# Six instead of three buffers for inverse degrees, residual rows and output rows in the pipelines after the two graph layers, with the output stores issued two steps later

## The reference, cut to what matters

```python
def _sage_layer(x, src, dst, deg_inv, Wl, bl, Wr):
    agg = segment_sum(x[src], dst) * deg_inv
    h = agg @ Wl.T + bl + x @ Wr.T
    norm = maximum(norm_of_row(h), EPS)
    return relu(h / norm)

h = _sage_layer(x, src, dst, deg_inv, Wl0, bl0, Wr0)
h = _sage_layer(h, src, dst, deg_inv, Wl1, bl1, Wr1)
out = layernorm(x + h)          # (v - mean) / sqrt(var + eps), over the 64 features
```

## Time and profile before

| what | us |
|---|---|
| median of 3 runs | 7693.83 |
| lowest and highest of them | 7691.86, 7711.77 |
| the profiled execution: its time | 7695.09 |
| the profiled execution: span from first to last instruction | 7693.3 |
| in it: edge stage of the first network and what precedes it, about | 0 to 5190 |
| node stage c, then the edge stage of layer 0, about | 5190 to 6406 |
| node stage after layer 0 | 6406 to 6492 |
| edge stage of layer 1 | 6492 to 7533 |
| node stage after layer 1, the last | 7533 to 7693.3 |

### The profile page before, as it was taken

The page is one execution under the profiler, slowest core; times in us unless marked ns, Lnnn a source line. Parts: engine busy times, 40 slices in busy tenths (PEclk is TensorE's granted clock), DMA queues, the critical chain, the costliest instruction groups (busy, mean ns, idle before and its releaser), DMA issues. The chain is left out here.

```text
span 7693.3 us, 142775 instructions
## 1 busy us (share of the span) xinstructions
PE 6764.5 (88%) x40296; PEld 5280.2 (69%) x40296; DVE 4537.4 (59%) x17372; ACT 2229.5 (29%) x4883; POOL 5906.4 (77%) x4715
## 2 busy tenths in 40 slices
PE   5998999989889998898999988987999996999993
PEld 4777877878778877787788877865555554555552
DVE  5777777777777777633333333336666664666663
ACT  2222222222222222222222222226333334333333
POOL 5888888888888888888888888864788784877873
PEclk7777777776777777766666677668999996999995
DMA  4333333333333333322222222223333334323342
GB/s 132 34 35 33 34 35 34 34 34 34 34 34 34 34 34 33 33 28 27 28 27 27 27 28 27 27 38 120 75 73 76 75 71 72 74 74 77 75 71 53
DMA packets 718022, 374.05 MB, mean 49 GB/s; under 512 B 550672, under 2 KB 668197, under 8 KB 717459
## 3 DMA queue, kind: packets, MB, share of 16 engines
q0 software_dynamic: 319648, 158.18, 20.6%
q1 hardware_dynamic: 395649, 210.89, 10.7%
q10 hardware_dynamic: 2482, 2.00, 0.1%
HBM read 289.60 MB, written 81.09 MB: 48 GB/s over the span
## 5 line engine op out<-in xcount | busy, mean ns | idle before, releaser
L665 POOL DMA_INDIRECT future<-sbuf,sidx x1564 | 2497.4, 1597 | 486.9 <-issue 453.8
L651 POOL DMA_INDIRECT gbuf<-in_x_dram,gidx x1564 | 1592.0, 1018 | 481.5 <-issue 471.9
L1571 PE MATMUL bank<-at_dst,rows 128*128 128x512 bf16 x3136 | 1204.9, 384 | 0.5 <-ACT rows L1538 0.5
L1573 PE MATMUL bank<-at_dst,rows 128*128 128x512 bf16 x3136 | 1201.9, 383 | 0.0
L1538 ACT CAST rows<-bank 128x384 bf16<-128x384 f32 x1568 | 751.2, 479 | 1224.8 <-PE bank L1557 1224.1
L1422 POOL DMA_INDIRECT gb<-x,nidx x640 | 794.1, 1241 | 243.2 <-issue 147.6
L1422 POOL DMA_INDIRECT gb<-h,nidx x640 | 781.5, 1221 | 245.7 <-issue 143.9
L1460 DVE TENSOR_SCALAR at_dst<-iota,metaf 128x512 bf16<-128x512 f16 x3136 | 942.2, 352 | 3.1 <-PE bank L1573 1.4
L977 PEld LDWEIGHTS bank<-w1pe,featT 96*128 96x128 f32 x3128 | 727.7, 271 | 308.6 <-issue 308.0
L978 PE MATMUL bank<-w1px,srcT 65*128 65x128 f32 x3128 | 820.7, 356 | 0.0
L977 PE MATMUL bank<-w1pe,featT 96*128 96x128 f32 x3128 | 820.7, 356 | 0.0
(11 more groups left out here) (260 smaller groups left out, 11120.4 us busy)
## 6 DMA issues: line engine op xcount, KB each, us to landing
laneb<-lanes SPq DMA_DIRECT2D x448, 224.0 KB
gbuf<-in_x_dram,gidx POOLq DMA_INDIRECT x1564
comb<-in_edge_attr_dram SPq DMA_DIRECT2D x391, 64.0 KB
future<-sbuf,sidx POOLq DMA_INDIRECT x1564, 3.2
blkb<-blkrow SPq DMA_DIRECT2D x240, 98.0 KB
future<-zero POOLq DMA_DIRECT2D x16, 800.0 KB, 17.9
fut<-future SPq DMA_DIRECT2D x100, 125.0 KB
gb<-x,nidx POOLq DMA_INDIRECT x644, 2.7
```

The source lines that it names most:

```text
L651: pool.indirect_dma_start(out=gbuf[:, b, q, :], out_offset=None, in_=x[:, :], in_offset=bass.IndirectOffsetOnAxis(ap=gidx[:, b, q:q + 1], ...
L665: pool.indirect_dma_start(out=future[q][:, :], out_offset=bass.IndirectOffsetOnAxis(ap=sidx[:, b, q:q + 1], axis=0), in_=sbuf[:, b, q, :], ...
L1571: pe.matmul(psHM[i % 2][:, :], rows16[:, j % AR, t % 2, 0:2 * D], at_dst[:, t % DR, :], start=(b == 0), stop=(b == BLOCKS - 1))
L1573: pe.matmul(psL[i % 2][:, :], rows16[:, j % AR, t % 2, 2 * D:4 * D], at_dst[:, t % DR, :], start=(b == 0), stop=(b == BLOCKS - 1)).then_in ...
```

## The change

Inverse degrees, residual rows and output rows get six buffers (`NL` = 6) where they had three; the waits that guard these buffers look back six chunks instead of three. `store_out` is placed at stage 10 of SP's list instead of 8. After layer 0 only the inverse degrees get more buffers, and `store_h` stays where it was. All other tiles keep three buffers, and no arithmetic changes.

```diff
+NL = 6
...
         def stored(sems, c, each=1):
-            return sems[c % NB], 16 * each * (c // NB)
+            return sems[c % len(sems)], 16 * each * (c // len(sems))
...
-                res, y, yc, ysq, tot, var, last_b = buffers(...)
+                res = tmp(f"{L}_res", [CP, NL, CQ * D])
+                last_b = tmp(f"{L}_last", [CP, NL, CQ * D])
+                y, yc, ysq, tot, var = buffers(...)
...
-            u_res = [tsem(f"{L}res{b}") for b in range(NB)]
-            u_st = [tsem(f"{L}st{b}") for b in range(NB)]
-            u_inv_ld = [tsem(f"{L}inv{b}") for b in range(NB)]
-            inv_b, = buffers(L + "i", ("inv", D, CH))
+            u_res = [tsem(f"{L}res{b}") for b in range(NL)]
+            u_st = [tsem(f"{L}st{b}") for b in range((NB, NL)[layer])]
+            u_inv_ld = [tsem(f"{L}inv{b}") for b in range(NL)]
+            inv_b = tmp(f"{L}_inv", [D, NL, CH])
...
                     def load_residual(c):
-                        if c >= NB:
-                            sp.wait_ge(u_y, c - NB + 1)
-                        sp.dma_start(res[:, c % NB, :], x1_c[c]).then_inc(u_res[c % NB], 16)
+                        if c >= NL:
+                            sp.wait_ge(u_y, c - NL + 1)
+                        sp.dma_start(res[:, c % NL, :], x1_c[c]).then_inc(u_res[c % NL], 16)
 
                     def load_inverse(c):
-                        if c >= NB:
-                            sp.wait_ge(u_scaled, c - NB + 1)
-                        sp.dma_start(inv_b[:, c % NB, :], chunk(invT, c)).then_inc(u_inv_ld[c % NB], 16)
+                        if c >= NL:
+                            sp.wait_ge(u_scaled, c - NL + 1)
+                        sp.dma_start(inv_b[:, c % NL, :], chunk(invT, c)).then_inc(u_inv_ld[c % NL], 16)
...
                     if layer == 0:
                         stages(load_inverse, None, None, None, store_h)
                     else:
-                        stages(load_inverse, load_residual, None, None, None, None, None, None, store_out)
+                        stages(load_inverse, load_residual, None, None, None, None, None, None, None, None, store_out)
...
                     def normal(c):
-                        if c >= NB:
+                        if c >= NL:
                             dve.wait_ge(*stored(u_st, c))
```

More of the change, by code:

```diff
@@ L1009, in stored @@
         def stored(sems, c, each=1):
-            return sems[c % NB], 16 * each * (c // NB)
+            return sems[c % len(sems)], 16 * each * (c // len(sems))
         def all_stored(eng, sems, each=1):
-            for b in range(NB):
-                eng.wait_ge(sems[b], 16 * each * len(range(b, CHUNKS, NB)))
+            for b in range(len(sems)):
+                eng.wait_ge(sems[b], 16 * each * len(range(b, CHUNKS, len(sems))))
         def by_slot(t):
@@ L1653, in build @@
             if layer == 1:
-                res, y, yc, ysq, tot, var, last_b = buffers(
-                    L, ("res", CP, CQ * D), ("y", CP, CQ * D), ("yc", CP, CQ * D), ("ysq", CP, CQ * D), ("tot", CP, CQ),
-                    ("var", CP, CQ), ("last", CP, CQ * D))
+                res = tmp(f"{L}_res", [CP, NL, CQ * D])
+                last_b = tmp(f"{L}_last", [CP, NL, CQ * D])
+                y, yc, ysq, tot, var = buffers(
+                    L, ("y", CP, CQ * D), ("yc", CP, CQ * D), ("ysq", CP, CQ * D), ("tot", CP, CQ),
+                    ("var", CP, CQ))
             (u_scaled, u_A, u_h, u_hsq, u_n, u_max, u_inv, u_rows, u_T, u_hT, u_y, u_tot, u_mean, u_yc,
              u_ysq, u_sd, u_rs, u_last) = [tsem(f"{L}u{i}") for i in range(18)]
-            u_res = [tsem(f"{L}res{b}") for b in range(NB)]
-            u_st = [tsem(f"{L}st{b}") for b in range(NB)]
-            u_inv_ld = [tsem(f"{L}inv{b}") for b in range(NB)]
-            inv_b, = buffers(L + "i", ("inv", D, CH))
+            u_res = [tsem(f"{L}res{b}") for b in range(NL)]
+            u_st = [tsem(f"{L}st{b}") for b in range((NB, NL)[layer])]
+            u_inv_ld = [tsem(f"{L}inv{b}") for b in range(NL)]
+            inv_b = tmp(f"{L}_inv", [D, NL, CH])
             psA = bank[0:2]
@@ L1683, in store_out @@
                         sp.wait_ge(u_last, c + 1)
-                        sp.dma_start(out_c[c], last_b[:, c % NB, :]).then_inc(u_st[c % NB], 16)
+                        sp.dma_start(out_c[c], last_b[:, c % NL, :]).then_inc(u_st[c % NL], 16)
                     if layer == 0:
@@ L1697, in scale @@
                             v = chunk(acc[0:D, :], c)
-                            pool.wait_ge(u_inv_ld[c % NB], 16 * (c // NB + 1))
-                            pool.tensor_tensor(v, v, inv_b[:, c % NB, :], ALU.mult).then_inc(u_scaled, 1)
+                            pool.wait_ge(u_inv_ld[c % NL], 16 * (c // NL + 1))
+                            pool.tensor_tensor(v, v, inv_b[:, c % NL, :], ALU.mult).then_inc(u_scaled, 1)
                         def clear_sums(c):
@@ L1720, in residual @@
                                 pool.wait_ge(u_yc, c - NB + 1)
-                            pool.wait_ge(u_res[b], 16 * (c // NB + 1))
+                            pool.wait_ge(u_res[c % NL], 16 * (c // NL + 1))
                             pool.wait_ge(u_rows, c + 1)
-                            pool.tensor_tensor(y[:, b, :], rows[:, b, :], res[:, b, :], ALU.add).then_inc(u_y, 1)
+                            pool.tensor_tensor(y[:, b, :], rows[:, b, :], res[:, c % NL, :], ALU.add).then_inc(u_y, 1)
                         def centre_y(c):
@@ L1780, in normal @@
                         dve.wait_ge(u_rs, c + 1)
-                        dve.tensor_tensor(by_slot(last_b[:, b, :]), by_slot(yc[:, b, :]), per_node(var[:, b, :]),
+                        dve.tensor_tensor(by_slot(last_b[:, c % NL, :]), by_slot(yc[:, b, :]), per_node(var[:, b, :]),
                                           ALU.mult).then_inc(u_last, 1)
```

## The result

The changed kernel took 7644.14 us as the median of 5 runs (7625.12 to 7657.27), the kernel before 7703.43 us in its 5 runs (7691.86 to 7711.77). The ratio is 0.9916 with a 95% interval of 0.9901 to 0.9932, so it is about 0.8% faster. The prediction was 7638 us, 7617 to 7652.

A forecast was written before the change was run, and what follows sets the result against it. After layer 1 POOL waits for inverse loads queued behind SP's residual load. Twenty steps falling from 6.33 to 3.6 us save 54.6, fill 2.1, less 1.1 for clears: 55.6 us less, 7638 us, range 7617 to 7652.

The forecast's parts named there:

- The wait and its cause: After layer 1, SP's residual load waits for y and holds the inverse load behind it; 3.5 us wait each step.
- The step: After layer 1: 3.67 us if POOL's scaling precedes DVE's `last`, 3.11 if `last` goes first; 3.6 taken, from 6.33.
- Why the scaling mostly goes first: After layer 1, POOL seems to win when its next instruction stands ready, favouring the 3.67 us step.
- `rows` of 7548.10: DVE instruction in the profile before, 1.87 us, passed while waiting by POOL's ready centring; taken as evidence on order.
- 3.11 us and 7628 us: Rival after layer 1: `last` goes ahead of the scaling, 3.11 us steps, 7628 us in all; chance 0.25.
- Fill: Start of the stage after layer 1: first centring no longer queued behind the late scaling; 2.1 us gained.
- The end: Fifteen more semaphore clears on SP, nine at the end, cost 1.1 us; steps after chunk 20's centring stay unchanged.
- The sum: Whole kernel: 54.6 us from 20 steps, plus 2.1 from fill, less 1.1 cost: 55.6 us less.
- the sign: Time ahead of the stage after layer 1: movement of the first 7533 us would show the forecast wrong.
- After layer 0, and the later store: Stage after layer 0 stays at 86 us, costed at nothing; nothing waits for the output store two steps later.

The follow-up runs named there:

- res_only: Six buffers for the residual rows alone, on the kernel before; 7635.60 us, ratio to before 0.9916.
- place_only: Kernel before with three buffers everywhere, the residual load moved from stage 1 to stage 3 of SP's list; 7646.72 us, ratio to before 0.9929.
- inv_only: Six buffers for the inverse degrees alone, on the kernel before; 7701.74 us, ratio to before 0.9999.
- noscale: The change with POOL's scaling after layer 1 cut to 4 of its 500 columns; 7641.50 us, ratio to before 0.9906.
- h_psum: The change with h kept in three PSUM banks instead of SBUF; 7632.57 us, ratio to before 0.9908.
- early_recip: The change with DVE taking the reciprocal for `last` ahead of h instead of behind it; 7650.33 us, ratio to before 0.9920.
- store8: The change with the output store back at stage 8 of SP's list; 7637.36 us, ratio to before 0.9926.
- last_first: The change with POOL's scaling of each chunk also waiting for `last` of six chunks before; 7650.43 us, ratio to before 0.9923.

## Why the prediction was right

**The wait and its cause.** Right, and shown: res_only and place_only each take all of it away, inv_only nothing.

**The step.** I had worked out 3.67 us for a step in which the scaling goes first and 3.11 for one in which `last` does, and taken 3.6. Measured: 3.66, 3.13 and 3.62. That the mean came out at 3.62 is partly luck: it is made of thirteen steps that tied one way, three that went the other way, and four others near the start, two of them longer than either; `last` didn't slip in "now and then" but only in the first seven steps. That DVE and POOL hold each other up is shown by noscale for `last`, and by h_psum for `rows` and y.

**Why the scaling mostly goes first.** Here the number was right by luck: the step of the argument that chose between 3.67 and 3.11 us failed. I took it from one `rows` of 7548.10, passed by a centring that stood ready, that a ready POOL instruction passes a waiting DVE one. In the change, in the thirteen steps in which `last` is held, the scaling starts 0.00 to 0.01 us ahead of it, in the three in which it isn't, `last` starts 0.02 to 0.03 us ahead, and in early_recip a waiting `last` goes ahead of a ready scaling (7590.90). What the Trainium skill states ("SBUF — State Buffer", section "Who interferes with whom") is that whoever issues first has the port, and I had given the row precedence; these steps agree with the page. By the page alone I would have said 3.11 us and 7628 us, which is further off: neither the page nor the row told that the two would tie and that the tie would mostly fall to the scaling. The range, 7617 to 7652, held both outcomes.

The `rows` of 7548.10 isn't alone. In inv_only the same instruction of the same chunk is passed by the centring again, and takes 2.01 us:

```profile
7549.27 1.23 POOL L1716 TENSOR_TENSOR acc<-acc,L__inv 64x500 f32<-64x500 f32 x1 [3.71 <-DMA L__inv<-invT]
7549.35 2.01 DVE L1762 SCALAR_TENSOR_TENSOR L__rows<-L__h,L__norm 125x256 f32<-125x256 f32 x1
7550.47 0.61 POOL L1732 TENSOR_TENSOR L__yc<-L__y,L__tot 125x256 f32<-125x256 f32 x1
```

So it repeats, and order of readiness isn't the whole rule. Why it happens there and not to `last` in early_recip stays open; no run tried it.

**Fill.** 2.1 us expected. From the first inverse load to the first centring it was 15.8 us (7549.08 - 7533.24) and is 13.7 (7534.00 - 7520.28): 2.1.

**The end.** 1.1 us for fifteen clears expected. After the centring of chunk 20 the stage takes 19.2 us instead of 17.6. Of these 1.6 us, 0.5 lie behind the last centring, where the nine clears are (0.06 us each, if all of it is theirs, against the 0.07 I took); 1.1 lie in the last four steps, 11.1 us instead of 10.1, which I had held to be unchanged. They seem to start from another phase of the two engines; I did not try it.

**The sum.** The stage: 54.3 from the steps, 2.1 from the fill, less 1.6, is 54.8 us; measured 160.1 - 105.2 = 54.9, predicted 55.6 for both stages. The profiled span fell by 67.8 us, and the other 13 us came ahead of the stage. I had named it as a sign of being wrong if the first 7533 us moved, and in this profile they did, by 13.0 us (the stage begins at 7520.28 instead of 7533.24), and by 15.4 already at the start of the stage after layer 0, ahead of everything that the change touches. When the same kernel was profiled again the stage began at 7538.98, 5.7 us later than before, and took 105.1 us (span 7644.1). So the beginning varies by itself, by as much as a third of the gain, and the sign was a poor one.

The forecast of 7638 was counted from the 7693.83 us of three runs; with five, the kernel before stood at 7703.43, and the medians are 59.3 us apart. That the forecast lay 6 us from the measured median owes something to this variation; what bears out the mechanism is the 54.9 us of the stage.

**After layer 0, and the later store.** Costed at nothing; 84.5 us before, 85.0 and 84.5 in the two profiles of the change (from 6410.32 to 6494.77 in the second), and store8 is level with the change.

## What to carry to other kernels

When a load is late, look in the issuing queue at what stands directly ahead of it: a wait there holds every transfer behind it. Here buffers for the late transfer gained nothing, while moving the waiting instruction two stages down the list gained as much as the whole change, at no memory. Before expecting a step to fall to the busiest engine's time, lay out which VectorE instructions with two SBUF inputs, or small scalar ones, meet a GpSimd instruction; here they kept a step at 3.6 us with no engine over 2.7 us of its own work. Putting one operand in PSUM took a whole instruction out of that contest. Such differences have to be read from the stage: whole runs of one kernel lay up to 40 us apart and don't show them.

## What the runs showed of the hardware

- A tie of 0.03 us or less between VectorE and GpSimd, settled the one way or the other, went with 0.53 us a step (3.66 against 3.13), and after a step that fell to GpSimd the same tie came again in the next: the kernel stayed in the slow pattern for the last thirteen of the twenty steps, in both profiles of the change.
- A VectorE instruction on 4 numbers a partition, 0.17 us alone, takes 0.56 us when it comes 0.08 us after a centring of 0.61 us, and 0.76 us when it comes into the middle of a scaling (1.04 us near its start, in last_first).
- A VectorE instruction with one input in PSUM and one in SBUF (`rows` with h in PSUM, 425 ns on average and none over 0.43 us, though it starts in the middle of a centring) was not held by GpSimd; with both in SBUF it took 699 ns on average.
- A waiting VectorE instruction went in ahead of a ready GpSimd instruction in early_recip (`last` at 7590.90), and was passed by one in two profiles (`rows`, 1.87 us before and 2.01 us in inv_only). What decides between the two isn't shown.
